# GpSimd builds the local keys' block-diagonal tiles unit by unit; first stacks by row half; 32-column value tiles; fewer warm-up matmuls

## The chip, the cores and the metric

One core of a Trainium2 chip, one launch. The metric is device time in microseconds. TensorE's clock has two levels, 2.4 and 1.2 GHz; the profile gives the granted share of the higher one.

## The reference

Two branches over four batches of 512 tokens, 128 wide, are added. The first is a chunked attention: 16 heads of 8, windows of 16 tokens, once over neighbouring tokens and once over every third token ("dilated", three residues), summed and projected:

```python
attn = softmax(einsum('bhqd,bhkd->bhqk', q, k) * SCALE)      # inside each window of 16
out = einsum('bhqk,bhkd->bhqd', attn, v)
return _linear(local_out + atrous_out, Wo, bo)
```

The second is a transformer block: low-rank attention over all 512 tokens, causal, 16 heads of 8 (half of each head rotated by position), then a shared expert and seven routed ones, of which each token takes two, as dense matmuls with weights:

```python
scores = where(causal, einsum('bqhd,bkhd->bhqk', qq, kk) * scale, -inf)
y = einsum('bhqk,bkhd->bqhd', softmax(scores), v) @ W_o
combined = einsum('tei,eih,te->th', silu(g) * u, Wd_r, wts) ; out = shared + combined
```

The kernel lays both into one stream of work and adds the results into `x`.

## The kernel before

The program is a list of steps that `plan()` builds; each engine walks the whole list and issues its own part of each step, so the list is the order of every queue. `merged()` interleaves several lists by the positions in `SPREAD`: a list with the range (lo, hi) has its items laid evenly between, and one unit is about one batch of scores. Semaphores between the parts do the rest.

*Front.* Batch 0 is led by `LN`, `WF` (folds two small weight matrices), `XT` (transpose of x), `MA`/`MB` (keys, side 0, and queries, side 1, of the full attention; `MB` is the turned half of the rotation, which VectorE multiplies and adds, L964 and L967), `ST`. `WARM` puts matmuls on a spare bank ahead of `WF`, `XT` and `MA`, two TensorE instructions each (L1182).

*Stacks.* A bf16 score is made exact by splitting q and k into three bf16 parts (L695 to L722: casts on ScalarE, VectorE or GpSimd, subtractions), and stacking products of parts along the 128 rows: rows 0 to 47 hold the terms of heads 0 to 7, rows 64 to 111 those of heads 8 to 15. SyncE stores the parts to DRAM with a broadcast, twelve DMAs a batch (three parts, two sides, two row halves, L576), and loads `k_stack` and `q_stack` back in `ST` (L587), 112 rows of 8 KB each. Batches alternate between two buffers.

*Scores.* Four groups of four heads a batch, eleven units each. `S` computes scores for the row maxima into a bank of ring A (two banks), drained by VectorE (L1000, L1004); after a group `SHIFT` puts the maxima into the stack. Two groups later `E` computes the shifted transposed scores into ring B (three banks), ScalarE takes the exponential (L823), and `PV` multiplies by the values: four heads side by side, head m in the 32 rows of bank_c from 32m, with 8 value columns and one of ones (L1265). `Y`, `YT`, `X1` take the result on.

*Local attention.* 34 pairs of windows are worked in five units of 8, 8, 8, 8 and 2. `LK`, `LQ`, `LV` project; GpSimd spreads k into `k_part` (L663, L665) and q into `q_part` (L679, L681). `k_diag` holds for each pair the keys times a head mask, eight masks x 1088 columns x two sides. In the `KD` steps VectorE makes four of the eight (L986) and ScalarE four (L772), each for all pairs, once the last `LS` of the batch before is done. `LS` multiplies q_part by k_diag into ring A, VectorE subtracts the maximum (`LS`, L1018 and L1021), ScalarE takes the exponential (`LR`), then `PT` transposes, `LO` multiplies by v_diag (loaded by `VD`), `LT` transposes back and `LW` projects.

*Norm and experts.* `R2` to `PICK` normalise and route; 32 expert steps `GU`/`DOWN` follow the scores. `late` reuses k_diag for their weights, loaded in `WX`.

The wait at the head of `LS` is for all of k_diag and q_part:

```python
if step[2] == 0:
    pe.wait_ge(k_diag_by_dve, KD_PARTS * (b + 1))
    pe.wait_ge(k_diag_by_act, KD_PARTS * (b + 1))
    pe.wait_ge(q_part_ready, KD_PARTS * (b + 1))
```

## Time and profile before

| | us |
|---|---|
| median of 3 runs | 449.01 |
| lowest, highest | 445.97, 450.13 |
| the profiled execution | 444.97 |
| its span in the profile | 443.2 |

The profile is of one execution. Its page gives busy time by engine, the span in 40 slices, the DMA queues, the chain of work that ended last, and the costliest groups of instructions; the trace answers for any stretch: a timeline, the waits, the chain, and windows with busy time and granted clock. PE is TensorE (PEld its weight loads), DVE VectorE, ACT ScalarE, POOL GpSimd, SP SyncE. The line numbers are those of the kernel above. An fp32 matmul is two TensorE instructions in the trace.

### The profile page before, as it was taken

How to read it: one execution, taken by the hardware profiler on the slowest of the kernel's cores; microseconds unless marked ns; L12 is line 12 of the kernel's file. 1: busy time of each engine (PE TensorE's matmuls, PEld its weight loads, DVE VectorE, ACT ScalarE, POOL GpSimd, SP SyncE). 2: the span in 40 equal slices, each digit the busy share in tenths (PEclk: the TensorE clock that was granted, in tenths of full speed). 3: DMA queues.
4: the chain of work that ended last, by engine and by line, in shares of the span. 5: the costliest groups of instructions: out<-in, count | busy, mean ns of one | idle time of the engine just before them, and what ended most of it. 6: DMA issues, size and time to landing. Idle time of an engine off the chain costs nothing.

```text
span 443.2 us, 11906 instructions
## 1 busy us (share of the span) xinstructions
PE 373.1 (84%) x4572; PEld 221.7 (50%) x4572; DVE 295.7 (67%) x854; ACT 224.9 (51%) x472; POOL 127.6 (29%) x148
## 2 busy tenths in 40 slices
PE   6834878885999969797987988889899999998894
PEld 6422635442466535364543654464443566655563
DVE  5865768794687896767879785866731345856542
ACT  5260227353566474464547544455544565566363
POOL 6374036263000354500336000000200235744244
PEclk9975989899899997999999996998955999999899
DMA  8274011036111116202037101230000000000000
GB/s 246 86 210 133 7 30 43 23 134 178 30 63 36 39 39 206 51 12 80 18 111 201 31 7 32 58 89 1 5 1 1 0 0 25 1 27 0 0 25 24
DMA packets 27390, 25.52 MB, mean 58 GB/s; under 512 B 11876, under 2 KB 25444, under 8 KB 26372
## 3 DMA queue, kind: packets, MB, share of 16 engines
q1 hardware_dynamic: 27336, 24.78, 19.4%
q8 instruction: 37, 0.61, 0.6%
q14 instruction: 17, 0.14, 0.1%
HBM read 14.64 MB, written 10.52 MB: 57 GB/s over the span
## 4 chain that ended last, share of the span: by engine, by line
PE 57%; DVE 24%; issue 9%; DMA 3%; ACT 3%; SPq 1%; POOL 1%; DVEq 0%; ACTq 0%
PE bank_B L1358 11%; PE bank_c L1265 8%; PE bank_B L1168 7%; PE bank_A L1364 6%; DVE differences L1000 6%; PE bank_A L1304 4%; PE bank_B L1174 3%; DVE s_loc L1021 2%; DVE row_max L1018 2%; PE bank_M L1211 2%; PE bank_M L1312 2%; DMA q_stack<-parts_dram 2%; PE bank_c L1182 2%; PE bank_M L1327 2%; DVE neg_max L1004 2%
## 5 line engine op out<-in xcount | busy, mean ns | idle before, releaser
L823 ACT ACTIVATE p_mla<-bank_B 128x512 f32<-128x512 f32 (+1 forms) x176 | 97.2, 561 | 94.1 <-PE bank_B L1174 92.9
L1000 DVE CUSTOM_DVE_ANT_0 differences<-masks,bank_A 128x512 bf16<-128x512 bf16 (+1 forms) x128 | 78.9, 616 | 32.6 <-PE bank_A L1151 23.6
L1168 PE MATMUL bank_B<-q_stack,k_stack 50*128 50x512 bf16 (+3 forms) x256 | 68.9, 324 | 25.8 <-DVE s_loc L1021 8.2
L1151 PE MATMUL bank_A<-k_stack,q_stack 48*128 48x512 bf16 (+3 forms) x256 | 66.3, 316 | 14.9 <-DMA q_stack<-parts_dram 11.0
L1358 PE MATMUL bank_B<-xrT,k_diag 128*128 128x512 f32 x128 | 64.0, 620 | 3.0 <-DVE k_diag L1129 3.0
L707 POOL TENSOR_TENSOR x<-x,q_part 128x512 f32<-128x512 f32 x32 | 40.7, 1273 | 79.5 <-ACT q_part L857 45.4
L1168 PEld LDWEIGHTS bank_B<-q_stack,k_stack 50*128 50x128 bf16 x256 | 20.1, 97 | 81.0 <-issue 41.7
L1174 PE MATMUL bank_B<-masks 64*128 64x64 bf16 (+1 forms) x512 | 54.0, 212 | 0.0
L1265 PE MATMUL bank_c<-p_mla,v_mla 128*9 128x128 f32 (+3 forms) x512 | 51.7, 479 | 0.7 <-ACT p_mla L823 0.4
L1174 PEld LDWEIGHTS bank_B<-masks 64*128 64x128 bf16 x512 | 42.8, 101 | 15.6 <-issue 4.0
L1129 DVE SCALAR_TENSOR_TENSOR k_diag<-k_diag,bank_B 128x512 f32<-128x512 f32 x32 | 22.0, 687 | 41.7 <-ACT k_diag L841 41.3
L857 ACT ACTIVATE q_part<-bank_A,expert_w 128x128 f32<-128x128 f32 x112 | 32.1, 370 | 30.3 <-PE bank_A L1364 30.3
L1364 PEld LDWEIGHTS bank_A<-k_diag 128*128 128x128 f32 x256 | 33.7, 195 | 14.8 <-issue 14.7
L1004 DVE TENSOR_REDUCE neg_max<-bank_A 128x2 f32<-128x512 f32 (+1 forms) x48 | 32.4, 687 | 8.6 <-PE bank_A L1159 7.8
L1364 PE MATMUL bank_A<-k_diag 128*128 128x128 f32 x256 | 34.6, 279 | 0.7 <-DVEq L1137 0.7
L621 POOL TENSOR_TENSOR nrm<-nrm,half 128x4 f32<-128x4 f32 (+2 forms) x6 | 10.0, 1658 | 82.6 <-DVE nrm L1080 79.8
L1358 PEld LDWEIGHTS bank_B<-xrT,k_diag 128*128 128x128 f32 x128 | 22.3, 197 | 21.0 <-issue 15.3
L719 POOL CAST parts<-rot 128x512 bf16<-128x512 f32 x6 | 4.1, 681 | 92.8 <-DVE rot L967 87.7
L1151 PEld LDWEIGHTS bank_A<-k_stack,q_stack 48*128 48x128 bf16 x256 | 18.7, 94 | 20.4 <-DMA q_stack<-parts_dram 11.2
L1134 DVE TENSOR_TENSOR k_diag<-bank_B,k_diag 128x512 f32<-128x512 f32 x32 | 22.1, 691 | 2.1 <-PE bank_B L1358 1.1
L1327 PE MATMUL bank_M<-v_diag,pT_loc 128*32 128x72 f32 x1088 | 22.9, 228 | 0.1
L1304 PE MATMUL bank_A<-k_diag,q_part 128*32 128x128 f32 x544 | 22.2, 300 | 0.5 <-DVE neg_max L1000 0.4
(149 smaller groups left out, 611.5 us busy)
## 6 DMA issues: line engine op xcount, KB each, us to landing
k_stack<-parts_dram SPq DMA_DIRECT2D x4, 896.0 KB, 7.2
q_stack<-parts_dram SPq DMA_DIRECT2D x4, 896.0 KB, 8.4
parts_dram<-parts SPq DMA_DIRECT2D x16, 192.0 KB, 2.4
v_dram<-v_rows SPq DMA_DIRECT2D x4, 648.0 KB, 4.1
parts_dram<-parts SPq DMA_DIRECT2D x16, 128.0 KB, 2.2
v_diag<-v_dram SPq DMA_DIRECT2D x32, 45.0 KB, 2.1
v_diag<-v_dram SPq DMA_DIRECT2D x32, 36.0 KB, 1.9
x<-in_x SPq DMA_DIRECT2D x4, 256.0 KB, 6.4
```

The source lines that it names most:

```text
L707: link(nc.gpsimd.tensor_tensor(x[:, tb, :], x[:, tb, :], weighted[down_no[step] % 2], ALU.add))
L823: drained_by(nc.scalar.activation(p_of(n)[:, m:m + len(heads), 0:w], src, ACT.Exp, scale=SCALE), step)
L857: ins = nc.scalar.activation(weighted[n % 2][:, i, :], down[:, i, :], ACT.Copy, scale=expert_w[:, c * NT + i, e - 1:e])
L1000: drained_by(nc.vector.tensor_tensor_reduce(differences[:, 0:w], masked16[:, S - w:], bank[:, 0:w], -1.0, -NEG, ALU.add, ALU.min, dst), step)
L1004: drained_by(nc.vector.tensor_reduce(dst, src, AX.X, ALU.max, negate=True), step)
L1151: return nc.tensor.matmul(bank_of(step)[:, n * w:(n + 1) * w], q_stack[b % 2][rows, h % 8, i * P:(i + 1) * P], k_stack[b % 2][rows, h % 8, ...
L1168: nc.tensor.matmul(bank_of(step)[:, m * w:(m + 1) * w], k_stack[b % 2][rows, h % 8, j * P:(j + 1) * P], q_stack[b % 2][rows, h % 8, j * P: ...
L1174: return nc.tensor.matmul(bank_of(step)[:, m * w:m * w + SLOT * (low + 1)], half_eye[half_of(4 * g), low, :], half_causalT[half_of(4 * g), ...
L1265: last = nc.tensor.matmul(bank_c[32 * m:32 * m + HD + 1, j * P:], v_mla[:, b % 2, j, 4 * g + m, :], p_of(n)[:, m, 0:S - j * P], start=(j = ...
L1304: last = nc.tensor.matmul(bank[PAIR * j:PAIR * j + PAIR, c:c + P], q_part[:, a, pair, :], k_diag[:, a, :, CHUNK * pair:CHUNK * pair + CHUN ...
L1358: full_by(nc.tensor.matmul(bank_of(use)[:], w_exp[:, e, m, :], x2T[:, c, :], start=True, stop=True), use)
L1364: last = nc.tensor.matmul(bank[:, i * D:(i + 1) * D], hid[n % 2][:, i * P:(i + 1) * P], w_exp[:, e, 2, :], start=True, stop=True)
```

## The change

- The first stacks: batch 0's stores go out in the order written below, and each stack is loaded in two halves, rows 0 to 63 in `ST 0`, the rest in a new step `ST2` after the last `LV` of batch 0; scores wait for the upper half (`upper_in`) from the third group on.
- From batch 1 on, the block-diagonal tiles are made by GpSimd in steps `KU(b,k)`, one for each unit, each as soon as `LS(b-1,k)` has read the old ones; `LS(b,k)` waits for its own. q_part is made in two steps `QD` (neighbouring, dilated). `KD` is left in batch 0 alone.
- The add of the rotation (L967) is GpSimd's from batch 1 on, in front of its split.
- `PV` uses stationary tiles of `PV_WIDTH` = 32 columns (the next heads' values fill the rows that nobody reads), narrower only at the end of the row for the last three heads.
- 12 instead of 56 warm-up instructions; the clearing of pT_loc moves behind batch 0's bias add; new positions in `SPREAD`.

```diff
-WARM = {("WF",): 14, ("XT", 0, 1): 8, ("MA", 0, 0): 6}
+WARM = {("WF",): 6}
...
-    "scores": [(-0.425, 4.13)],
-    "local": [(-0.415, 0.151), (0.682, 1.537), (1.566, 2.55), (2.462, 3.111)],
-    "project": [(-0.241, 0.196), (0.2, 1.358), (1.405, 2.134)],
-    "stacks": [(-0.922, -0.922), (0.514, 0.514), (1.48, 1.48), (2.141, 2.141)],
-    "values": [(-2.253, -2.253), (0.262, 0.262), (1.367, 1.367), (3.099, 3.099)],
-    "norm": [(1.467, 1.901), (2.152, 2.731), (3.484, 3.677), (4.411, 4.977)],
-    "experts": [(3.974, 5.368)],
-    "statistics": [(-1.535, -1.535)],
+    "scores": [(-0.374, 4.13)],
+    "local": [(-0.216, 0.445), (0.405, 1.245), (1.418, 2.322), (2.432, 3.229)],
+    "project": [(-0.303, 0.196), (0.38, 1.129), (1.609, 2.2)],
+    "stacks": [(-0.955, -0.955), (0.515, 0.515), (1.113, 1.113), (2.221, 2.221)],
+    "values": [(-2.111, -2.111), (0.293, 0.293), (1.494, 1.494), (2.046, 2.046)],
+    "norm": [(1.467, 1.768), (2.121, 2.653), (3.622, 4.014), (4.338, 4.715)],
+    "experts": [(4.075, 5.103)],
+    "spreads": [(0.232, 0.532), (0.558, 1.703), (1.912, 2.578)],
+    "statistics": [(-0.503, -0.503)],
...
-            if k == NLU - 1:
-                steps += [("KD", b + 1, n) for n in range(KD_PARTS)] if b + 1 < B else [("WX",)]
+            if k == NLU - 1 and b + 1 == B:
+                steps.append(("WX",))
...
+    def spreads(b):
+        steps = []
+        for k in range(NLU):
+            steps.append(("KU", b, k))
+            if k in (LOCAL_UNITS - 1, NLU - 1):
+                steps.append(("QD", b, int(k == NLU - 1)))
+        return steps
...
+                if step == ("ST", 0):
+                    for side, part, hp in ((0, 0, 0), (0, 0, 1), (0, 1, 0), (0, 2, 0), (1, 0, 0), (1, 1, 0), (1, 2, 0)):
+                        if part < 2:
+                            sp.wait_ge(rounded[side], part + 1)
+                        else:
+                            sp.wait_ge(split_ready, side + 1)
+                        store(0, side, part, hp)
+                    sp.wait_ge(rows_out, 16 * 4)
+                    sp.wait_ge(parts_out[0][0], 16 * 3)
+                    load(0, 0, slice(0, SLOT), stacks_in[0])
+                    for part in (1, 2):
+                        store(0, 0, part, 1)
+                    sp.wait_ge(parts_out[1][0], 16 * 3)
+                    load(0, 1, slice(0, SLOT), stacks_in[0])
+                if kind == "ST2":
+                    for part in range(3):
+                        store(0, 1, part, 1)
+                    for side in range(2):
+                        sp.wait_ge(parts_out[side][1], 16 * 3)
+                        load(0, side, slice(SLOT, SLOT + SHIFT_ROW), upper_in)
...
+                if step[0] == "KU":
+                    _, b, k = step
+                    wait_full(pool, ("LS", b - 1, k))
+                    if k == 0:
+                        pool.wait_ge(heads_in, 16)
+                        pool.wait_ge(k_part_ready, b + 1)
+                    pairs = LUNITS[k][0]
+                    c = slice(CHUNK * pairs[0], CHUNK * (pairs[-1] + 1))
+                    w = c.stop - c.start
+                    for a in range(2):
+                        ins = nc.gpsimd.tensor_tensor(k_diag[:, a, :, c],
+                                                      k_part[:, a, c].unsqueeze(1).broadcast_to((P, X, w)),
+                                                      head_mask[:].unsqueeze(2).broadcast_to((P, X, w)), ALU.mult)
...
                 if step[0] == "MB" and step[1] > 0:
...
-                    pool.wait_ge(rot_ready, n)
+                    whole = rot[:, side, :]
+                    wait_drained(pool, ("MA", b, side))
+                    wait_drained(pool, step)
+                    link(nc.gpsimd.tensor_tensor(whole, whole, turned[b][:], ALU.add))
+                    pool.sem_inc(rot_ready, 1)
...
+                    heads = v_mla[:, b % 2, j].rearrange("p h d -> p (h d)")
                     for m in range(4):
-                        last = nc.tensor.matmul(bank_c[32 * m:32 * m + HD + 1, j * P:], v_mla[:, b % 2, j, 4 * g + m, :],
+                        first = (HD + 1) * (4 * g + m)
+                        width = min(PV_WIDTH, H * (HD + 1) - first)
+                        last = nc.tensor.matmul(bank_c[32 * m:32 * m + width, j * P:], heads[:, first:first + width],
...
-                    if step[2] == 0:
-                        pe.wait_ge(k_diag_by_dve, KD_PARTS * (b + 1))
-                        pe.wait_ge(k_diag_by_act, KD_PARTS * (b + 1))
-                        pe.wait_ge(q_part_ready, KD_PARTS * (b + 1))
+                    if b:
+                        pe.wait_ge(k_diag_by_pool, NLU * (b - 1) + step[2] + 1)
+                    elif step[2] == 0:
+                        pe.wait_ge(k_diag_by_dve, KD_PARTS)
+                        pe.wait_ge(k_diag_by_act, KD_PARTS)
+                    if step[2] in (0, LOCAL_UNITS):
+                        pe.wait_ge(q_part_ready, 2 * b + (2 if step[2] else 1))
```

In the new list `KU(1,0)` is ahead of the eighth score unit of batch 0's third group, `LS(1,0)` after the third of the fourth; `MB(1,0)` and `MB(1,1)` stand at the end of the second group and after the second unit of the third; `KU(3,1)`, `MB(3,0)` and, some three units on, `MB(3,1)` follow each other at the turn of batch 2's second and third group. The first `GU` comes after all `E`.

## Rows read from the trace of the kernel before

**Rows 1.** The page: busy time, chain by engine, one DMA issue line
```profile
PE 373.1 (84%) x4572; PEld 221.7 (50%) x4572; DVE 295.7 (67%) x854; ACT 224.9 (51%) x472; POOL 127.6 (29%) x148
PE 57%; DVE 24%; issue 9%; DMA 3%; ACT 3%; SPq 1%; POOL 1%; DVEq 0%; ACTq 0%
q_stack<-parts_dram SPq DMA_DIRECT2D x4, 896.0 KB, 8.4
```

**Rows 2.** Timeline to the first scores: start, duration, engine, line, operation [idle before]
```profile
18.12 8.88 SPq L576 DMA_DIRECT2D parts_dram<-parts  x12
35.40 0.17 DVE L886 TENSOR_TENSOR nrm<-mv,nrm 128x12 f32<-128x12 f32 x1
37.35 1.03 PE L1151 MATMUL bank_A<-k_stack,q_stack 48*128 48x512 bf16 x2 [11.01 <-DMA q_stack<-parts_dram]
38.00 0.69 DVE L1000 CUSTOM_DVE_ANT_0 differences<-masks,bank_A 128x512 bf16<-128x512 bf16 x1 [2.43 <-PE bank_A L1151]
```

**Rows 3.** Timeline at the front: warm-up matmuls and VectorE ahead of WF
```profile
3.97 5.39 PE L1182 MATMUL bank_c<-eye 128*128 128x128 f32 x28 [3.97 <-DMA eye<-in_c_eye]
8.87 1.11 DVE L945 TENSOR_SCALAR xr<-x,mv,nrm 128x128 f32<-128x128 f32 x4
```

**Rows 4.** Timeline: two waits of TensorE, and a KD multiply beside GpSimd's split
```profile
163.36 1.76 DVE L986 TENSOR_SCALAR k_diag<-k_part,head_mask 128x1088 f32<-128x1088 f32 x1
110.76 0.58 PE L1168 MATMUL bank_B<-q_stack,k_stack 50*128 50x512 bf16 x1 [4.65 <-issue]
180.21 0.37 PE L1168 MATMUL bank_B<-q_stack,k_stack 50*128 50x512 bf16 x1 [1.87 <-issue]
```

**Rows 5.** Chain of waits by line, first 66 to 77 us, then 228 to 244
```profile
by line: DVE k_diag L986 25.5%; DVE neg_max L1004 14.3%; issue 10.9%; PE bank_M L1289 9.8%; PE bank_M L1206 9.6%; DVE differences L1000 6.7%; ACT pT_loc L805 6.0%; PE bank_M L1312 5.5%; PE bank_A L1304 4.1%; DVE row_max L1018 3.9%; DVE s_lo
...
by line: DVE differences L1000 19.8%; DVE k_diag L986 15.0%; issue 14.1%; DVE neg_max L1004 11.7%; PE bank_c L1265 8.8%; DVE xn L1088 3.4%; DVE xn L1080 3.3%; PE bank_B L1168 3.1%; DVE s_loc L1021 2.7%; DVE nrm L1085 2.5%; PE bank_M L1336 2
```

**Rows 6.** Windows: stretch, length, busy PE, PEld, DVE, ACT, POOL, granted clock, DMA, GB/s
```profile
28.00:36.00 8.00, 0.00 (x0) 0.00 (x0) 7.43 (x31) 4.79 (x5) 5.40 (x9) 0.54 0.97 268
110.70:115.00 4.30, 4.24 (x27) 1.57 (x27) 2.03 (x7) 2.14 (x4) 0.00 (x0) 0.61 0.00 0
162.70:166.20 3.50, 0.00 (x0) 0.00 (x0) 3.47 (x9) 0.88 (x2) 3.27 (x4) 0.86 0.01 1
166.20:172.00 5.80, 5.73 (x31) 3.00 (x31) 1.95 (x9) 1.99 (x6) 2.48 (x5) 0.50 0.39 136
302.00:320.00 18.00, 15.43 (x222) 7.71 (x218) 14.50 (x48) 11.70 (x23) 2.29 (x2) 1.00 0.01 3
322.00:342.00 20.00, 20.00 (x108) 7.99 (x106) 4.87 (x29) 9.15 (x17) 0.00 (x0) 0.51 0.01 1
```

**Rows 7.** Groups by line and shape: GpSimd's multiply, copy, subtract; two weight loads
```profile
L1304 PEld LDWEIGHTS bank_A<-k_diag,q_part 128*32 128x32 f32 x544 | 16.6, 120 | 5.0 <-issue 2.1 <-DVE neg_max L1000 1.9
L720 POOL TENSOR_TENSOR rest<-rot,parts 128x512 f32<-128x512 f32 x6 | 7.0, 1159 | 0.5
L1265 PEld LDWEIGHTS bank_c<-p_mla,v_mla 128*9 128x9 f32 x512 | 7.7, 89 | 7.4 <-ACT p_mla L823 1.6 <-issue 0.8
L681 POOL COPY q_part<-qT 64x288 f32<-64x288 f32 x8 | 5.7, 718 | 0.5
L643 POOL TENSOR_TENSOR xr<-xn,nrm 128x512 f32<-128x512 f32 x3 | 3.1, 1039 | 23.2 <-issue 22.5 <-POOL parts L722 0.7
```

**Rows 8.** Chain of waits: by line 322 to 342 us, pieces there, two at full clock
```profile
by line: PE bank_c L1265 32.3%; PE bank_B L1168 30.7%; PE bank_B L1358 18.6%; PE bank_B L1174 15.7%; PE bank_M L1272 5.2%
...
335.21 1.82 PE bank_c L1265 x8
338.58 3.71 PE bank_B L1358 x4
...
99.66 0.98 PE bank_c L1265 x8
247.55 0.92 PE bank_A L1304 x32
```

More of the change, by code:

```diff
@@ L57 @@
 P_RING = 2
+PV_WIDTH = 32
 PT_RING = 1
@@ L235, in plan @@
     steps = first[:1] + [("WF",)] + lead + [("ST", 0)]
-    steps += [step for step in first[1:] if step not in lead] + [("KD", 0, n) for n in range(KD_PARTS)]
+    rest = [step for step in first[1:] if step not in lead]
+    after = 1 + max(n for n, step in enumerate(rest) if step[0] == "LV")
+    rest.insert(after, ("ST2", 0))
+    steps += rest
+    steps += [("KD", 0, n) for n in range(KD_PARTS)] + [("QD", 0, n) for n in range(2)]
     at = SPREAD
@@ L249, in plan @@
     assert all(at["PICK", b] < at["DOWN", b, 1] and at["X1", b] < at["R2", b] for b in range(B))
+    assert all(at["LQ", b] < at["KU", b, 0] and at["LS", b - 1, k] < at["KU", b, k] < at["LS", b, k]
+               for b in range(1, B) for k in range(NLU))
+    assert all(at["LS", b - 1, (LOCAL_UNITS - 1, NLU - 1)[n]] < at["QD", b, n] < at["LS", b, (0, LOCAL_UNITS)[n]]
+               for b in range(1, B) for n in range(2))
+    assert all(at["KU", b - 1, NLU - 1] < at["LK", b] and at["QD", b - 1, 1] < at["LQ", b] for b in range(2, B))
     return steps
@@ L438, in build @@
         v_zeroed, v_rows_set = sem("v_zeroed"), sem("v_rows_set")
-        parts_out = [sem(f"parts_out{side}") for side in range(2)]
+        parts_out = [[sem(f"parts_out{side}{hp}") for hp in range(2)] for side in range(2)]
+        upper_in = sem("upper_in")
         rows_out = sem("rows_out")
@@ L524, in load_x, with store, load @@
                 sp.dma_start(x[:, b * NT:(b + 1) * NT, :], xv[:, b]).then_inc(x_in[b], 16)
+            def store(b, side, part, hp):
+                terms = STORES[side][part]
+                nt = len(range(*terms.indices(TERMS)))
+                to = parts_dram[b % 2, side, hp, 0:SHIFT_ROW, :].rearrange("(t d) (a n) -> (d a) t n", d=HD, n=S)
+                sp.dma_start(to[:, terms, :], parts[hp::2, side, part:part + 1, :]
+                             .broadcast_to((SLOT, nt, S))).then_inc(parts_out[side][hp], 16)
+            def load(b, side, rows, done):
+                dst = (q_stack if side else k_stack)[b % 2]
+                src = parts_dram[b % 2, side].rearrange("h r n -> (h r) n")
+                sp.dma_start(dst[rows].rearrange("p a n -> p (a n)"), src[rows, :]).then_inc(done, 16)
             load_x(0)
@@ L573, in _ @@
[L573 removed]
                         for hp in range(2):
[L575 to L578 removed]
+                            store(b, side, part, hp)
@@ L579, in _ @@
+                if kind == "ST" and b:
                     if b >= 2:
                         wait_full(sp, ("E", b - 2, GROUP_ORDER[-1], NT - 1, 0))
-                    else:
-                        sp.wait_ge(rows_out, 16 * 4)
                     for side in range(2):
-                        sp.wait_ge(parts_out[side], 16 * 6 * (b + 1))
-                        dst = (q_stack if side else k_stack)[b % 2]
-                        src = parts_dram[b % 2, side].rearrange("h r n -> (h r) n")
-                        sp.dma_start(dst[0:SLOT + SHIFT_ROW].rearrange("p a n -> p (a n)"),
-                                     src[0:SLOT + SHIFT_ROW, :]).then_inc(stacks_in[b % 2], 16)
+                        for hp in range(2):
+                            sp.wait_ge(parts_out[side][hp], 16 * 3 * (b + 1))
+                        load(b, side, slice(0, SLOT + SHIFT_ROW), stacks_in[b % 2])
@@ L767, in _ @@
                         act.wait_ge(heads_in, 16)
[L768 to L770 removed]
+                        act.wait_ge(k_part_ready, 1)
                     x = KD_PARTS + n
@@ L964, in _ @@
                     drained_by(nc.vector.tensor_tensor(dst, bank[:], rope[:, which, :], ALU.mult), step)
-                    if which:
+                    if which and b == 0:
                         wait_drained(dve, step)
@@ L1222, in _ @@
                         pe.wait_ge(stacks_in[b % 2], STACK_IN * (b // 2 + 1))
+                    if b == 0 and step[2] == 2 * PER_GROUP:
+                        pe.wait_ge(upper_in, STACK_IN)
                     if step not in waits_for_e:
```

80 lines of the change are left out of this document (40 added, 40 removed).

## The prediction

> **What bounds the kernel now.** I read the page's busy line, its chain, then windows of 2 to 20 us, the waits of TensorE, and the timeline around each. TensorE is busy 84% of the span and makes up 57% of the chain, VectorE 24% [rows 1]: no engine is full, and the order of the steps decides. The reader should see four kinds of loss. (a) Start: TensorE stands 11.01 us until q_stack lands and first works at 37.35; VectorE's first drain of a score bank is at 38.00 [rows 2]. (b) At the first scores of batches 1 and 2 TensorE waits 4.65 and 1.87 us [rows 4]; the row names no releaser, but these are the moments at which the q_stack loads of 8.4 us land [rows 1]. (c) The four `KD` steps put 1088 columns eight times into the queues of VectorE and ScalarE, between score banks that TensorE waits for. `KD` on VectorE is 25.5% of the chain from 66 to 77 us and 15.0% from 228 to 244 [rows 5]; in the third batch's stage TensorE does nothing for 3.5 us beside a busy VectorE and then runs 5.8 us at granted clock 0.50 (1.2 GHz) [rows 6]. (d) The end of the scores: from 322 to 342 TensorE is busy 20.00 of 20.00 us at a clock of 0.51, ScalarE only 9.15 [rows 6], and the chain there names no other engine [rows 8]. The experts behind it are dense TensorE work at full clock, and the change takes nothing from them.
>
> **Part by part.** Sums are against the profiled execution, 444.97 us with a span of 443.2; the median shown is 449.01, so I carry the difference over to it.
>
> *First stacks by row half.* Twelve stores are issued one after the other for 8.88 us, then two loads of 112 rows (896 KB); q_stack's lands at 37.3 [rows 1, 2]. Afterwards only seven stores go ahead of the lower k half (64 rows, 512 KB) and two more ahead of the lower q half. At 8.88 / 12 = 0.74 us an issue lower q is reached near 18.12 + 10 x 0.74 = 25.5 and waits for its stores to land, I take 26.5; 1.0 MB at the 268 GB/s of that stretch [rows 6] is 3.8 us, landed near 31 to 32. The remaining three stores, v_dram and the upper halves (heads 8 to 15, needed from group 2) lie behind, under some 20 us of scores. But VectorE is not free: `KD` and `STATS 0` keep it until 35.57 [rows 2]. So the first drain moves from 38.00 to 35.6: **-2.4 us** (0 to -4).
>
> *Warm-up matmuls.* 44 of 56 instructions go. The 28 ahead of `WF` took 5.39 us, but VectorE's own work ahead of `WF` runs to 9.98 [rows 3], so `WF` is drained only some 0.5 us earlier; the 28 later ones stood between it and `MA`, which can start about 2 us earlier, possibly at 1.2 GHz, where each `MA`/`MB` costs 0.86 us more. **0** (-2 to +1).
>
> *Stacks of batches 1 and 2.* `MA`/`MB` of batch 1 move from group 2 to the turn of groups 1 and 2 of batch 0, and `ST 2` forward by more than a group. The 4.65 us wait should go, with the slow stretch after it (4.24 us of work at 0.61, worth 1.7 at full clock), and the 1.87 us wait too [rows 4, 6]. -6.3 and -1.9.
>
> *Block-diagonal tiles.* Twelve `KD` steps leave VectorE and ScalarE. What they cost on the chain is 0.255 x 11 = 2.8 us and 0.150 x 16 = 2.4 us in two stages [rows 5], and in the third 3.5 us idle plus half of 5.8 us at half clock, 6.4 [rows 6]. -11.6. The second half of `MB`'s rotation (one add in six steps) also leaves VectorE. GpSimd gets per full unit two multiplies of 8 x 128 elements per partition. No row has them; the nearest is its 512-element multiply with a broadcast operand, 1039 ns, 2.0 ns an element, the high bound its copy of 288 elements at 718 ns, 2.5 [rows 7]. I take the multiply: 2 x 1024 x 2.03 = 4.2 us a full unit (high 5.1), 18 us a batch, 54 in all. GpSimd is at 29% (127.6 us), and in the score stages mostly waits.
>
> *What the new work can hold up.* `LS(b,k)` on TensorE now waits for its own unit, with all scores queued behind it. The tightest place is batch 1: between `KU(1,0)` and `LS(1,0)` stand seven to eight score units, at (320 - 37) us / 176 units = 1.6 us each about 12 us, against 4.2 + 4.2 + four q copies of at most 0.72, 11.3 us: 0 to +5, I take +1. In batch 3 `KU(3,1)` stands just ahead of `MB(3,0)` on GpSimd, whose add and split are three two-input instructions of 1.16 us and two casts, I take 5 us [rows 7]; VectorE waits for that split in `MB(3,1)` about three units later, with score drains behind it. 4.2 + 5 less 5 us: +3 (0 to +4).
>
> *Wider value tiles.* The stationary side goes from 9 to 32 columns; the moving columns are as before. A 9-column weight load takes 89 ns, a 32-column one 120 ns [rows 7]: 0 to 8 x 31 ns x 64 `PV` = 16 us. In `LS` 32 matmuls of 128 columns with 32-column loads take 0.92 us together [rows 8], so the loads hide; near the low end, +1. What it may bring is loss (d). A `PV` of 512 queries takes 0.98 us at full clock and 1.82 in the slow stretch; the clock came back only after one `GU` step, four instructions with 128-column weights, 3.71 us at half clock [rows 8]. I forecast that with 32-column tiles this stretch runs at 1.0. Then its 16.4 us of E and PV (322.1 to 338.5) fall to about 11 (half is 8.2, but ScalarE needs about 9 and TensorE would wait for it), and 3.7 us of `GU` to 1.9: **-7.3** (0 to -9).
>
> The Trainium skill ("TensorE: Matmul & The Clock Gate", Part 1 and the goals table) holds that keeping TensorE busy without gaps releases the clock. In this row a TensorE without a gap stays at 0.51, so the trace disagrees; by that rule the width of a tile buys nothing, which is the rival "the clock stays low", 434 us. The skill's "SBUF — State Buffer" (contention rules) says that a GpSimd instruction that reads SBUF locks out VectorE instructions in a two-port mode, and this speaks against the change. The trace has a `KD` multiply of 1.76 us beside GpSimd's split [rows 4], and agrees as far as that goes; by the rule some of the 28 normalising multiplies of VectorE would be held up by as much as one GpSimd multiply, 2 us.
>
> **Sum.** Mid stages -6.3 - 1.9 - 11.6 = -19.8, of which I keep three quarters, -15, since time given free is partly taken by the next wait (VectorE is busy 14.50 of 18 us there [rows 6]). With the local work of batch 0 laid more evenly I add -2. -2.4 - 15 - 2 - 7.3 + 1 + 1 + 3 = -21.7. 444.97 becomes 423.3; on the median 449.01, **427 us**.
>
> **Rivals.**
> *The freed engines buy little.* TensorE is the pace wherever it isn't idle; only its idle gaps with their slow stretches go, 6.3 + 1.9 + 6.4, and half comes back elsewhere, while batch 0's local work, pushed back, costs about 6 us of TensorE time later. For it: busy 15.43 of 18 us at full clock [rows 6]. -2.4 - 7 + 6 - 7.3 + 5 = -6: 443. If the clock doesn't rise either, 449.
> *No net change:* that case, within 1%.
> *Slower: GpSimd becomes the pace.* Place: `KU` in batches 1 to 3. From `KU(1,0)` to `LS(1,4)` lie about 35 units, 56 us, less about 15 us of GpSimd's other work; five units fit up to 8 us each. At 12 us a unit (5.9 ns an element) TensorE stands about 20 us more a batch, net +25 with the gains: 474; it decides from 8 us on, and 10 us gives about 455. Against it: the three GpSimd rows shown cost 2.0 to 2.5 ns an element [rows 7].
> *The clock stays low:* 427 + 7 = 434. For it: nothing in this trace shows a wide `PV`.
> *More than forecast:* all mid gains kept and the stages more even, 415.
>
> **Chances.** Forecast (420 to 432) 0.40; clock stays low, 434, 0.17; more than forecast, 415, 0.18; freed engines buy little, 443, 0.08; no change 0.09; slower 0.08. The predicted time is the likeliest case's. The range takes in the three cases next to it and leaves out the ends: 412 to 443. About 1% is what a measurement of this kernel can tell from no change: faster 0.82, within 1% 0.10, slower 0.08.
>
> **What would show it.** First drain of a score bank near 35.6; no TensorE wait above 1 us at the first S of batches 1 and 2; `KU` multiplies near 2.1 us; no long wait of TensorE for GpSimd's k_diag at `LS`, and a VectorE wait of some 3 us at `MB(3,1)`; granted clock near 1.0 and a 512-query `PV` near 1 us between the last S and the first GU. Wrong it would be if GpSimd's multiplies take over 4 us, if the slow stretches only move, or if the wider loads show between the value matmuls.

## The result, and the profile after

The changed kernel takes **432.02 us** (median of 4 runs, 428.61 to 433.03), the kernel before 449.57 in the same comparison (445.97 to 451.45): a ratio of **0.961**, 95% interval 0.952 to 0.969. The profiled execution took 432.39 us, its span is 430.6. Set against the profiled execution of before the gain is only 12.6 us, since that one (444.97) was among the quicker ones. Over all comparisons of this study the kernel before ran 54 times, from 436.30 us at a mean granted clock of 0.929 to 452.96 at 0.906, and the changed one 10 times with a median of 431.8. The difference of the means is 15.0 ± 2.0 us (2.2 standard errors, as wherever "±" stands below). So differences of 2 to 3 us between two kernels here are at the edge of what can be told. The experiments ran in four sets on four chips, in which the kernel before had medians of 448.0, 449.1, 447.9 and 444.3; the changed kernel itself ran again only in the second, so a difference between two sets carries more than its "±". Where only the fast executions count (within 1.5% of a kernel's fastest in the set), the ratio to the kernel before is 0.985 (0.978 to 0.992) for batch 2's normalisation alone, 1.004 (0.997 to 1.011) for the other places alone and 1.016 (1.006 to 1.025) for wide value tiles alone.

The page of the changed kernel, busy time and chain by engine:

```profile
PE 365.3 (85%) x4528; PEld 220.1 (51%) x4528; DVE 287.7 (67%) x836; ACT 211.3 (49%) x460; POOL 181.5 (42%) x184
PE 56%; DVE 17%; issue 6%; ACT 4%; POOL 3%; DMA 2%; SPq 2%; DVEq 0%; ACTq 0%; POOLq 0%
```

Beside [rows 1]: GpSimd has 53.9 us more and VectorE's share of the chain fell from 24% to 17%; but VectorE is only 8.0 us less busy. Twelve multiplies of `KD` and six adds of the rotation are gone from it: by the groups of both kernels these lines took 15.6 + 4.1 us, and 3.5 are left of them, 16.2 us less. Half of that came back, most of it in three groups whose number of instructions is the same: the multiplies of `LN` take 6.7 instead of 4.6 us, those of `R3` 6.5 instead of 5.7, the `rt` products of `PICK` 4.5 instead of 2.5.

The start, in the timeline of the changed kernel:

```profile
32.12 1.03 PE L1219 MATMUL bank_A<-k_stack,q_stack 48*128 48x512 bf16 x2 [6.43 <-DMA q_stack<-parts_dram]
34.55 0.68 DVE L1068 CUSTOM_DVE_ANT_0 differences<-masks,bank_A 128x512 bf16<-128x512 bf16 x1
35.30 0.61 PE L1219 MATMUL bank_A<-k_stack,q_stack 48*128 48x512 bf16 x1 [2.15 <-DVE neg_max L1068]
```

TensorE starts 5.2 us earlier than in [rows 2], VectorE's first drain comes 3.45 earlier, and TensorE then waits 2.15 us for VectorE, as forecast.

From the first drain to the last S the two kernels take nearly the same time. The windows of before and of the changed kernel (start, end, length, then busy PE, PEld, DVE, ACT, POOL, the granted clock, DMA share, GB/s):

```profile
38.00:315.70 277.70, 234.88 (x3786) 137.51 (x3787) 209.00 (x615) 141.05 (x277) 61.02 (x84) 0.94 0.22 62
```

```profile
34.55:311.30 276.75, 238.00 (x3785) 142.08 (x3787) 200.17 (x589) 127.98 (x264) 116.49 (x119) 0.92 0.24 64
```

Idle TensorE went from 42.8 to 38.8 us, but busy TensorE rose by 3.1 at a lower clock. Behind the last S lie 127.5 us before and 119.3 after. So in these two executions the end gave 8.2 us, the start 3.4, and the middle, where the change does most and where 13 us net were forecast, 1.0.

What stands in the middle instead are new waits. The groups by line and shape of the changed kernel:

```profile
L727 POOL TENSOR_TENSOR k_diag<-k_part,head_mask 128x1024 f32<-128x1024 f32 x24 | 45.6, 1899 | 2.5 <-POOLq L716 0.5 <-POOL q_part L750 0.2 <-POOL x L690 0.2
L1020 DVE TENSOR_SCALAR xn<-x,mv,nrm 128x128 f32<-128x128 f32 x12 | 6.7, 622 | 0.0
```

and its timeline at two places:

```profile
92.32 4.50 DVE L1020 TENSOR_SCALAR xn<-x,mv,nrm 128x128 f32<-128x128 f32 x4
92.62 3.87 POOL L727 TENSOR_TENSOR k_diag<-k_part,head_mask 128x1024 f32<-128x1024 f32 x2 [0.18 <-POOL q_part L750]
97.35 1.47 PE L1380 MATMUL bank_A<-k_diag,q_part 128*32 128x128 f32 x32 [3.31 <-DVE neg_max L1068]
...
193.21 7.88 POOL L727 TENSOR_TENSOR k_diag<-k_part,head_mask 128x1024 f32<-128x1024 f32 x4 [0.27 <-POOLq L716]
193.25 1.90 DVE L1187 TENSOR_TENSOR rt<-rt 128x32 f32<-128x32 f32 x1
196.16 0.39 PE L1236 MATMUL bank_B<-q_stack,k_stack 50*128 50x512 bf16 x1 [3.05 <-DVE neg_max L1072]
```

The reader should see an instruction of VectorE that takes many times its length while GpSimd multiplies: the four normalising multiplies of `LN 2`, 1.11 us together elsewhere ([rows 3] has the same work at the front), take 4.50; the small `rt` product of `PICK 0`, 0.19 us undisturbed (e1_hold, below), takes 1.90, which is one `KU` multiply (1899 ns). The score drains queue behind, and TensorE stands 3.31 and 3.05 us. Behind the second wait it runs slowly, by the windows:

```profile
196.00:200.00 4.00, 3.28 (x45) 2.05 (x49) 3.23 (x11) 2.19 (x4) 3.84 (x3) 0.61 0.14 28
200.00:210.00 10.00, 10.00 (x122) 5.64 (x118) 3.56 (x11) 4.74 (x10) 1.09 (x1) 0.64 0.01 2
```

The Trainium skill ("SBUF — State Buffer", the contention rules) says that a VectorE instruction with two SBUF inputs contends with a GpSimd instruction that reads SBUF. The `rt` product is such a one, and this trace agrees with 1.90 against 0.19 us.

### The profile page after: what moved, and what is told of

Read it like the earlier page. It is cut to its first block, busy times and chain, and to the rows that moved or that the text cites. A ratio compares the mean times of both kernels' runs of the same rounds, so it can differ in the third digit from the quotient of the medians.

```text
span 430.6 us, 11866 instructions
## 1 busy us (share of the span) xinstructions
PE 365.3 (85%) x4528; PEld 220.1 (51%) x4528; DVE 287.7 (67%) x836; ACT 211.3 (49%) x460; POOL 181.5 (42%) x184
## 4 chain that ended last, share of the span: by engine, by line
PE 56%; DVE 17%; issue 6%; ACT 4%; POOL 3%; DMA 2%; SPq 2%; DVEq 0%; ACTq 0%; POOLq 0%
PE bank_B L1434 12%; PE bank_c L1338 7%; PE bank_A L1440 6%; PE bank_B L1236 6%; DVE differences L1068 4%; PE bank_A L1380 4%; PE bank_M L1403 3%; PE bank_M L1279 2%; ACT p_mla L893 2%; PE bank_M L1388 2%; PE bank_B L1242 2%; PE bank_M L1274 2%; PE bank_M L1362 1%; PE bank_M L1269 1%; PE bank_A L1219 1%
## 5 line engine op out<-in xcount | busy, mean ns | idle before, releaser
L1236 PE MATMUL bank_B<-q_stack,k_stack 50*128 50x512 bf16 (+3 forms) x256 | 65.5, 310 | 16.4 <-DVE neg_max L1068 5.3
L1219 PE MATMUL bank_A<-k_stack,q_stack 48*128 48x512 bf16 (+3 forms) x256 | 67.5, 322 | 11.7 <-DMA q_stack<-parts_dram 6.4
L1434 PE MATMUL bank_B<-xrT,k_diag 128*128 128x512 f32 x128 | 61.7, 603 | 3.3 <-DVE k_diag L1197 3.3
L1242 PE MATMUL bank_B<-masks 64*128 64x64 bf16 (+1 forms) x512 | 51.5, 206 | 0.0
L727 POOL TENSOR_TENSOR k_diag<-k_part,head_mask 128x1024 f32<-128x1024 f32 (+1 forms) x30 | 49.3, 1642 | 2.9 <-POOLq L716 0.5
L1338 PE MATMUL bank_c<-p_mla,v_mla 128*32 128x384 f32 (+13 forms) x512 | 47.7, 446 | 2.0 <-ACT p_mla L893 1.1
L1242 PEld LDWEIGHTS bank_B<-masks 64*128 64x128 bf16 x512 | 40.5, 96 | 14.1 <-issue 2.3
L1072 DVE TENSOR_REDUCE neg_max<-bank_A 128x2 f32<-128x512 f32 (+1 forms) x48 | 32.6, 690 | 10.4 <-PE bank_A L1227 9.5
L784 POOL TENSOR_TENSOR rot<-rot,rest 128x512 f32<-128x512 f32 x6 | 7.6, 1271 | 59.6 <-DVE rest L1034 59.4
L1403 PE MATMUL bank_M<-v_diag,pT_loc 128*32 128x72 f32 x1088 | 24.1, 238 | 1.0 <-DMA v_diag<-v_dram 0.7
```

Source lines behind the costliest of these rows:

```text
L727: ins = nc.gpsimd.tensor_tensor(k_diag[:, a, :, c], k_part[:, a, c].unsqueeze(1).broadcast_to((P, X, w)), head_mask[:].unsqueeze(2).broadc ...
L1219: return nc.tensor.matmul(bank_of(step)[:, n * w:(n + 1) * w], q_stack[b % 2][rows, h % 8, i * P:(i + 1) * P], k_stack[b % 2][rows, h % 8, ...
L1236: nc.tensor.matmul(bank_of(step)[:, m * w:(m + 1) * w], k_stack[b % 2][rows, h % 8, j * P:(j + 1) * P], q_stack[b % 2][rows, h % 8, j * P: ...
L1242: return nc.tensor.matmul(bank_of(step)[:, m * w:m * w + SLOT * (low + 1)], half_eye[half_of(4 * g), low, :], half_causalT[half_of(4 * g), ...
L1338: last = nc.tensor.matmul(bank_c[32 * m:32 * m + width, j * P:], heads[:, first:first + width], p_of(n)[:, m, 0:S - j * P], start=(j == 0) ...
L1403: last = nc.tensor.matmul(bank[PAIR * j:PAIR * j + PAIR, c:c + w], pT_loc[:, t % PT_RING, par, 2 * i + (g ^ par), PAIR * j:PAIR * j + PAIR ...
```

## The experiments

Each is a small edit. Medians are given with lowest and highest; the kernel before ran beside each set. Two theories on the missing middle were set against each other: that GpSimd's multiplies hold VectorE up (called the lock below), and that time freed on VectorE is simply worth little.

**Holding GpSimd back (e1_hold).** Two waits in `KU` on GpSimd:

```
 wait_full(pool, ("LS", b - 1, k))
+if (b, k) == (1, 2):
+    pool.wait_ge(xn_ready, 3)
+if (b, k) == (3, 0):
+    pool.wait_ge(picked, 1)
```

> The changed kernel with two waits more on GpSimd: the tile unit KU(1,2) waits until VectorE has normalised batch 2 (step LN 2), and KU(3,0) until PICK 0 is done. Lock theory (the middle stages gained 0.9 us instead of 13 because GpSimd's tile multiplies hold up VectorE's small SBUF-to-SBUF instructions, 3.31 and 3.05 us of idle TensorE and half-clock stretches behind them): the four multiplies of LN 2 take 1.1 to 1.4 us together instead of 4.50, the rt instruction of PICK 0 0.2 us instead of 1.90, both TensorE waits go, and the time falls by 5 to 9 us, to about 425. Rival (time freed on VectorE is worth little, another wait sets the pace): the instructions get short but the time stays at 431 to 433. Second rival (the slowness has nothing to do with GpSimd): the instructions stay long.

425.59 us (420.45 to 429.60, 6 runs), 6.2 ± 3.1 less than the changed kernel. The timeline of this kernel at the same two places:

```profile
90.62 1.11 DVE L1024 TENSOR_SCALAR xn<-x,mv,nrm 128x128 f32<-128x128 f32 x4
91.88 3.87 POOL L731 TENSOR_TENSOR k_diag<-k_part,head_mask 128x1024 f32<-128x1024 f32 x2 [1.18 <-DVE xn L1024]
92.27 1.08 PE L1384 MATMUL bank_A<-k_diag,q_part 128*32 128x128 f32 x32
...
191.51 0.19 DVE L1191 TENSOR_TENSOR rt<-rt 128x32 f32<-128x32 f32 x1
192.06 7.82 POOL L731 TENSOR_TENSOR k_diag<-k_part,head_mask 128x1024 f32<-128x1024 f32 x4 [0.86 <-DVE expert_w L1193]
192.71 0.39 PE L1240 MATMUL bank_B<-q_stack,k_stack 50*128 50x512 bf16 x1 [1.34 <-DVE neg_max L1076]
```

GpSimd does all of its work, only some of it 1 us later, and it costs nothing there. 1.11 for 4.50 us, 0.19 for 1.90; no wait before the `LS`, and 1.34 for 3.05. From 192 to 207 us the clock is 1.00, where the changed kernel had 0.61 and 0.64 behind the wait, and the last S comes at 303.4 instead of 311.3 us. The lock theory is right, in place and size.

**Without the multiplies (e2_ku_out).** `KU`'s two multiplies replaced by `pool.sem_inc(k_diag_by_pool, 1)`.

> The changed kernel without GpSimd's multiplies in KU (the local keys' block-diagonal tiles stay those of batch 0; the semaphores are still raised), so that 49 us of GpSimd work are gone and nothing takes their place. Lock theory: 8 to 10 us less than the changed kernel, about 423, with no VectorE multiply of LN above 0.5 us. Rival (freed time is worth little): 430 to 432. If GpSimd's own queue were what is late (its split, its q copies): also faster, but then the holding of KU in the other run would not help.

424.03 us (421.49 to 426.63), 7.6 ± 2.6 less than the changed kernel and 1.6 below e1_hold in the median, which can't be told from nothing. So 49 us of GpSimd work cost 6 to 8 us, and all that can be shown of it lies at those two places. This kernel leaves the local keys' tiles of batches 1 to 3 unmade.

**Writing alone (e11_ku_memset).** The multiplies replaced by `nc.gpsimd.memset(k_diag[:, a, :, c], 0.25)`.

> The changed kernel with KU's two multiplies replaced by two memsets of the same slices of k_diag, so GpSimd writes the same bytes and reads nothing; the local attention of batches 1 to 3 is computed from a constant. Lock theory with reading as its cause: the four multiplies of LN 2 take 1.4 us together, 0.34 us each, though a GpSimd memset runs beside them, and the time is that of the kernel without KU multiplies, 424. Rival (any long GpSimd access holds VectorE up, writing too): LN 2's multiplies take as long as the memset beside them lets them, over 2 us together, and 426 to 431.

421.60 us (418.07 to 423.89, 4 runs), not to be told from the run without the multiplies (2.7 ± 3.5 less). The timeline of this kernel at `PICK 0`, then its group of memsets:

```profile
185.22 3.98 POOL L727 MEMSET k_diag<- 128x1024 f32 x4 [0.24 <-POOLq L716]
185.29 0.19 DVE L1185 TENSOR_TENSOR rt<-rt 128x32 f32<-128x32 f32 x1
```

```profile
L727 POOL MEMSET k_diag<- 128x1024 f32 x24 | 22.8, 951 | 1.9 <-POOLq L716 0.5 <-POOL q_part L748 0.2 <-POOL x L690 0.2
```

This is the same `rt` product, begun 0.07 us after GpSimd's first memset of 951 ns: 0.19 us. Beside a multiply it was 1.90. So GpSimd's reading is what holds this instruction up, not its writing. For `LN 2` the run says nothing: there the memsets end at 89.02, before VectorE's multiplies begin at 90.68, so the rival (writing holds such multiplies up too) stays untested.

**Tiles back on VectorE and ScalarE (e3_after_kd).** The step order gets `KD` back in `local`, `KU` goes, and the rotation's add returns to VectorE:

```
-            if k == NLU - 1 and b + 1 == B:
-                steps.append(("WX",))
+            if k == NLU - 1:
+                steps += ([("KD", b + 1, n) for n in range(KD_PARTS)] + [("QD", b + 1, n) for n in range(2)]
+                          if b + 1 < B else [("WX",)])
...
-        lists.append((spreads(b), *at["spreads"][b - 1]))
```

> The changed kernel with the block-diagonal tiles of batches 1 to 3 and the second half of the rotation back on VectorE and ScalarE, everything else (front, order of the other steps, wide value tiles, warm-ups) as changed. Prediction as it stands: +11.6 for the KD steps and nothing back, 444. Lock theory: +11.6 for the KD steps, -6 to -9 for the lock that goes: 435 to 438. Rival (freed engine time is worth little): the lock goes and the KD steps hide, 424 to 429.

441.40 us (439.15 to 446.17), 10.4 ± 2.7 more than the changed kernel and 16.7 ± 3.5 more than e1_hold. The second number is the worth of the tiles without the lock. The prediction as it stands (+11.6) fits the first better than what the lock theory expected (435 to 438): the lock theory had taken 11.6 for the tiles too, and by the second number they are worth more. Where it lies, in windows of this kernel at its second `KD`:

```profile
88.00:92.00 4.00, 2.26 (x24) 0.69 (x21) 3.93 (x7) 4.00 (x6) 3.79 (x4) 0.63 0.02 5
92.00:96.00 4.00, 4.00 (x53) 2.83 (x50) 2.69 (x5) 2.36 (x4) 3.52 (x7) 0.51 0.54 183
```

VectorE and ScalarE are full (3.93 and 4.00 of 4 us), TensorE has 2.26, and then works 4.00 of 4.00 us at clock 0.51: the idle time is paid twice. It need not be. The windows of e9_before_order (below), which has the same four steps at the same moment:

```profile
88.00:92.00 4.00, 3.07 (x62) 2.25 (x66) 4.00 (x7) 4.00 (x5) 3.69 (x6) 1.00 0.52 180
92.00:96.00 4.00, 3.50 (x89) 2.42 (x77) 3.79 (x13) 3.75 (x10) 1.36 (x3) 1.00 0.07 20
```

TensorE finds more to do there beside full VectorE and ScalarE (3.07 of 4 us instead of 2.26), and no slow stretch follows. The two kernels have the same places in the step order up to there; they differ in the front, in the width of the value tiles and in how q_part is made. Which of these lets TensorE work on isn't shown.

**Narrow value tiles (e4_narrow).** `PV_WIDTH = HD + 1` instead of 32 in the changed kernel.

> The changed kernel with value tiles of 9 columns as before, all else as changed. Width theory: granted clock near 0.5 between the last S and the first GU, 512-query PV 1.8 us there, and 7 to 9 us more, about 440. Rival (the clock is up there because of the order or because an idle gap comes earlier or later): clock 1.0 and the time within 1 us of 432.

432.19 us (427.85 to 435.69), 0.6 ± 2.8 more than the changed kernel: nothing. The windows over the end of the scores and the first GU, changed kernel first, then with 9 columns:

```profile
320.00:340.00 20.00, 18.66 (x158) 10.79 (x156) 8.17 (x36) 11.45 (x22) 1.27 (x1) 1.00 0.01 2
```

```profile
320.00:340.00 20.00, 18.80 (x155) 10.97 (x156) 8.79 (x37) 10.89 (x21) 1.27 (x1) 1.00 0.01 2
```

Clock 1.00 in both, where the kernel before had 0.51 in a like stretch [rows 6]. The clock is up, as forecast, but not through the width.

**Wide value tiles alone (e5_before_wide).** The kernel before with the changed `PV` lines and nothing else.

> The kernel before with value tiles of 32 columns and nothing else. The run with 9-column tiles in the changed kernel (432.2 us, granted clock 1.00 between the last S and the first GU) spoke against the width. Width theory (the forecast's step): granted clock about 1.0 from 322 to 342 us and 7 us less than before, 441. Order theory (what lifts the clock in the changed kernel is where batch 2's transposes and router stand): clock about 0.5 there as before, a 512-query PV 1.8 us, time as before, 448 +- 3.

451.64 us (447.76 to 454.28): 4.7 ± 2.5 more than the kernel before over all its runs, 2.6 in the medians of this set. The windows from the last S to the first GU, kernel before first, then with wide tiles:

```profile
315.70:338.50 22.80, 22.16 (x173) 10.37 (x167) 8.01 (x40) 12.10 (x24) 1.58 (x2) 0.64 0.01 1
```

```profile
319.90:342.80 22.90, 22.30 (x173) 10.77 (x167) 8.01 (x40) 12.13 (x24) 1.58 (x2) 0.64 0.01 1
```

Clock 0.64 in both, so the width doesn't lift it. The time lies just above what the order theory allowed (448 ± 3). Why the kernel gets slower by the width is open; the windows show TensorE busy 240.4 of 282.1 us between first drain and last S against 234.9 of 277.7, at 0.92 against 0.94.

**Batch 2's normalisation later (e6_before_norm).** One pair of numbers in the kernel before:

```
-    "norm": [(1.467, 1.901), (2.152, 2.731), (3.484, 3.677), (4.411, 4.977)],
+    "norm": [(1.467, 1.901), (2.152, 2.731), (3.622, 4.014), (4.411, 4.977)],
```

> The kernel before with batch 2's normalisation, transposes, router and PICK at the changed kernel's place (0.14 and 0.34 groups later, after the last S and among the E units), nothing else. Order theory: the stretch between the last S and the first GU runs at a granted clock near 1.0 and the time falls by about 7 us, to 441. Rival (the clock there hangs on what came long before, as on the waits and stages of the whole kernel): clock 0.5 somewhere in the stretch, 448.

438.09 us (437.14 to 438.88): 8.5 ± 1.5 less than the kernel before, the largest gain of any single edit to that kernel. Its window from the last S to the first GU, then its timeline:

```profile
318.50:334.40 15.90, 15.11 (x176) 8.07 (x169) 7.54 (x39) 11.62 (x24) 2.29 (x2) 1.00 0.01 3
```

```profile
328.97 0.66 PE L1201 MATMUL bank_M<-eye,xn 128*128 128x128 f32 x4
331.06 0.96 PE L1347 MATMUL bank_M<-wide,xrT 128*128 128x7 f32 x8
332.30 1.04 PE L1265 MATMUL bank_c<-p_mla,v_mla 128*9 128x512 f32 x8
334.38 1.95 PE L1358 MATMUL bank_B<-xrT,k_diag 128*128 128x512 f32 x4 [0.17 <-ACT p_mla L823]
```

The same work that took 22.8 us at 0.64 takes 15.9 us at 1.00, with 9-column tiles; a `PV` of 512 queries takes 1.04 us and the first GU 1.95, where before they took 1.82 and 3.71 [rows 8]. From the last S to the end it is 117.1 us instead of 127.5. In the kernel before, the transposes (L1201) and the router (L1347) of batch 2 stood at 318.18 and 319.75, just ahead of the fall at 322; here they stand ten microseconds later and no fall follows. In the kernel before TensorE was busy 5.36 of 6 us before the fall, and busy throughout after it. Of that kernel one execution is traced, and 14 of its 54 took no more than 442.8 us: whether its clock falls at 322 us in every one isn't shown.

**The other places (e9_before_order).** The kernel before with the changed kernel's numbers for scores, local, project, stacks, values and statistics; norm of batches 2 and 3 and the experts stay.

> The kernel before with all of the changed kernel's places in the step order (local, project, stacks, values, statistics, first group of scores) except batch 2's and 3's normalisation and the experts, which stay. What is known: the changed kernel with KD put back stands at 441.4 us, and order of the normalisation (-11) and the front (-3.4 at the first drain) would alone give about 434.6. Forecast of the prediction (the 4.65 and 1.87 us waits at the first S of batches 1 and 2 go, and local work lies more evenly): 8 to 10 us less than before, 439 to 441. Theory now (the new places cost more TensorE time at half clock and idle than these waits did, as long as KD sits on VectorE and ScalarE): 452 to 458, although both waits are gone. Between, 447 to 451: the 6.8 us come from the joint, not from the order.

442.57 us (439.36 to 449.51, 12 runs): 3.0 ± 3.2 less than the kernel before in this set, 5.3 in the medians. The theory (452 to 458) fell, and so did the value between. A gain isn't shown clear of noise, and 8 to 10 us, the forecast's size, is too much. In its trace (of the execution of 449.51 us) the wait at the first S of batch 1 is 1.56 us instead of 4.65 [rows 4]. At that of batch 2 there is still one, of 2.12 us for VectorE. The changed kernel has its like; its timeline there:

```profile
173.71 1.21 DVE L1156 TENSOR_SCALAR xn<-x,nrm 128x128 f32<-128x128 f32 x4
174.85 0.68 DVE L1086 TENSOR_REDUCE row_max<-bank_A 128x32 f32<-128x512 f32 x1
175.56 0.69 DVE L1089 TENSOR_TENSOR s_loc<-bank_A,row_max 128x512 f32<-128x512 f32 x1
176.31 0.55 PE L1236 MATMUL bank_B<-q_stack,k_stack 50*128 50x512 bf16 x1 [1.73 <-DVE s_loc L1089]
```

The stacks are there in time now, but VectorE is busy without a gap from `R3 0` to the local maxima just ahead of it, and TensorE waits 1.73 us for VectorE where it had waited 1.87 for the load.

**First stacks whole again (e12_whole).** The changed kernel with twelve stores and two loads of 112 rows:

```
-                    load(0, 0, slice(0, SLOT), stacks_in[0])
-                    for part in (1, 2):
-                        store(0, 0, part, 1)
-                    sp.wait_ge(parts_out[1][0], 16 * 3)
-                    load(0, 1, slice(0, SLOT), stacks_in[0])
...
+                        load(0, side, slice(0, SLOT + SHIFT_ROW), stacks_in[0])
```

> The changed kernel with the first stacks stored and loaded whole as before (twelve stores, then two loads of 112 rows), all else as changed. The forecast's step says +2.4 us (first drain of a score bank back near 38.0 from 34.5, at most +3.5), 434 to 435. Rival (the start at half clock gives it back: the first scores run at 0.50 and TensorE is behind anyway): 431 to 432. Rival (later scores meet the clock in another place, as in the other runs, where single waits cost twice their length): 436 to 440.

433.83 us (429.69 to 435.54), 1.6 ± 2.6 more than the changed kernel, which ran in other sets. Against the kernel before of its own set it is 10.8 ± 4.0 less, where the changed kernel was 15.0 ± 2.0 less, which would make the halves worth 4. The timeline:

```profile
35.83 1.03 PE L1211 MATMUL bank_A<-k_stack,q_stack 48*128 48x512 bf16 x2 [10.80 <-DMA q_stack<-parts_dram]
36.47 0.69 DVE L1060 CUSTOM_DVE_ANT_0 differences<-masks,bank_A 128x512 bf16<-128x512 bf16 x1 [2.51 <-PE bank_A L1211]
```

The drain at 36.47 is 1.92 us later than with halves, and both differences in time are in line with that. In the kernel before it stood at 38.00, so 1.5 of the 3.45 us came from the rest of the front (fewer warm-ups, the memset of `pT_loc` moved); which of them, no run parts.

**Warm-ups in the wait for the stacks (e7_hold_warm).** e1_hold with `WARM = {("WF",): 6, ("S", 0, 0): 40}`.

> The changed kernel with the two GpSimd waits (425.6 us) and 40 warm-up matmuls on the idle TensorE ahead of the first S, while the stacks are still loading. In that kernel the scores run at granted clock 0.50 from 32 to about 49 us and TensorE is busy nearly throughout from 44. If TensorE's idle time ahead of the first S is what holds the clock down: clock 1.0 from 32 us on, last S 2 to 4 us earlier, 422 to 424. Rival (the score units themselves don't keep it up, or VectorE sets the pace there anyway): 425 to 426, and 427 if the extra matmuls delay the first S.

421.31 us (420.21 to 425.03): 3.2 ± 3.2 less than e1_hold, at the edge; against the kernel before of the same set a ratio of 0.950, interval 0.941 to 0.958. It is the fastest kernel of this study that leaves nothing out. Its windows:

```profile
34.00:36.00 2.00, 1.36 (x7) 0.45 (x6) 1.46 (x5) 0.00 (x0) 1.46 (x1) 1.00 0.88 160
36.00:38.00 2.00, 0.72 (x2) 0.18 (x2) 1.71 (x6) 0.00 (x0) 2.00 (x1) 1.00 1.02 119
...
40.00:42.00 2.00, 1.07 (x3) 0.31 (x4) 1.86 (x9) 0.00 (x0) 0.08 (x1) 0.50 0.00 0
```

The clock is 1.00 when the scores begin, but VectorE sets the pace there (TensorE is busy 0.72 of 2 us), and from 40 us on the clock is 0.50 again. The warm-ups take 9.10 us and end at 34.4, so the first S comes 3 us later than in e1_hold. The gain, if it is one, isn't at the start: the first drain is at 34.79 against 34.47.

**Batch 0's local work earlier (e10_hold_warm_local).** e7_hold_warm with `"local": [(-0.415, 0.151), ...` as in the kernel before.

> The kernel with two GpSimd waits and 40 warm-up matmuls (421.3 us), with batch 0's local work at the place that it had before (0.2 to 0.3 of a group earlier). If pushing it back was what cost time (TensorE busy at granted clock 0.50 from 40 to 48 us with nothing but scores, clock 1.00 in the kernel before from 48 us on, where local work lay there): 2 to 4 us less, 417 to 419. Rival (VectorE is what the first scores wait for, and local work there only adds to its queue): 421 to 425.

435.05 us (430.55 to 436.46): 12.2 ± 2.6 more than e7_hold_warm, and neither theory expected it. Its timeline:

```profile
31.19 1.94 PE L1384 MATMUL bank_A<-k_diag,q_part 128*32 128x128 f32 x32 [6.08 <-ACT k_diag L846]
33.06 9.97 PE L1254 MATMUL bank_c<-eye 128*128 128x128 f32 x80
42.96 0.39 PE L1223 MATMUL bank_A<-k_stack,q_stack 48*128 48x512 bf16 x1
43.38 0.69 DVE L1072 CUSTOM_DVE_ANT_0 differences<-masks,bank_A 128x512 bf16<-128x512 bf16 x1 [8.00 <-PE bank_A L1223]
...
101.24 1.93 PE L1384 MATMUL bank_A<-k_diag,q_part 128*32 128x128 f32 x32 [4.51 <-POOLq L757]
```

`LS(0,0)` now stands ahead of the first S, and TensorE waits 6.08 us there for ScalarE's `KD`. The 40 warm-ups come behind it in the queue: they no longer fill that wait but follow it, for 9.97 us, and the first drain is at 43.38 instead of 34.79. So 8.6 us of the loss lie at the start. The stacks were there in time (the lower q half, issued at 26.17, lands 5.0 us later), and without warm-ups TensorE would have been free for the first S at 33.06. The edit doesn't part the place of the local work from the warm-ups, and what an earlier place costs by itself isn't shown. Later TensorE waits 4.51 us at `LS(1,0)` for GpSimd's q copies, which stand behind two units of `KU`; this is the wait that the prediction priced at 0 to +5, and the changed kernel doesn't have it.

**The changed kernel again (e8_after_again).**

> The changed kernel unaltered, for its time beside the others of this set and for a second trace. All theories: 430 to 433 us; the 4.50 us of LN 2's multiplies and the clock 1.00 from 320 to 340 us come back.

431.83 us (427.41 to 434.62, 6 runs); the groups by line show `LN`'s multiplies again at 6.7 us for 12, and the clock from 320 to 340 us is again 1.00. Both traces of the changed kernel show the same.

## Why the prediction was right, and where not

The forecast, 427 us with 412 to 443, holds the 432.0, and faster was right. But one gain was put down to the wrong edit, and that another edit of the same change gave about as much is luck. One loss was named but not counted; it is about the 5 us by which 427 fell short. Point by point, against [rows 1 to 8] as the steps used them.

- **First stacks by half, -2.4.** First drain 34.55 instead of the 35.6 forecast: the bound was read off the end of `STATS 0` in [rows 2], 35.57, and VectorE came there 0.94 us earlier. Undone alone the edit is worth 1.6 ± 2.6, and 1.92 us at the first drain; the other 1.5 of the 3.45 us come from the rest of the front, for which the forecast had nothing. Right within that. Whether local work has to move back for it, no run shows: in e10_hold_warm_local the warm-ups spoil the answer.
- **Warm-ups, 0.** Not undone by itself, so not shown. Forty new ones ahead of the first S gave 3.2 ± 3.2.
- **Stacks of batches 1 and 2, -6.3 and -1.9, and more even local work, -2.** The 4.65 us wait [rows 4] is gone in the changed kernel; the 1.87 one has its like in 1.73 us for VectorE at the same S. The step that failed here is "and the 1.87 us wait too": it asked when the load lands and not what VectorE has just ahead of that S. All order edits but the normalisation gave 3.0 ± 3.2 where 0.75 x 8.2 + 2 = 8.2 were forecast: the sum of these terms is too high, by how much stays open. And the first wait comes back when all ahead of it gets quicker: in e1_hold TensorE waits 3.10 us at the first S of batch 1, so `ST 1` is the next step to move.
- **Tiles off VectorE and ScalarE, -11.6 (of which the sum keeps three quarters, 8.7).** Worth 10.4 ± 2.7 as the change has them. The term was mis-sized all the same: without the lock they are worth 16.7 ± 3.5. What it left out is the slow stretch that can follow a `KD` gap (clock 0.51 from 92 to 96 us in e3_after_kd) at the first two batches; it had counted one only at the third [rows 6].
- **A unit of `KU` 4.2 us, 54 in all.** 1899 ns for 1024 elements, 1.86 ns each where 2.03 was taken from [rows 7]; 3.8 us a unit, 49.3 in all. Right. GpSimd as the pace (the rival on the slow side, from 8 us a unit) was far off, as argued.
- **New waits, +1 at `LS(1,0)` and +3 at `MB(3,1)`.** Neither came in the changed kernel. At `LS(1,0)` TensorE does wait, 3.31 us, but for VectorE's drain behind the held multiplies of `LN 2`; the wait for GpSimd's own work shows only in e10_hold_warm_local (4.51 us). VectorE's waits for GpSimd in the changed kernel are only those for the roots:

```profile
DVE nrm L962 <- POOL nrm L666: 3.0, 2, 1.8
...
DVE nrm L1153 <- POOL nrm L666: 1.1, 1, 1.1
```

- **The lock, "up to 2 us" and not in the sum.** This is the step that failed in the middle: a cost put at nothing in the sum. It cost 6.2 ± 3.1: the price of one held instruction is the GpSimd multiplies beside it (1.90 for one; 3.39 for the four of `LN 2`, 4.50 less 1.11), and on top of it come the drains queued behind and half-clock work (0.61 and 0.64 from 196 to 210). The forecast had seen the sign of it in [rows 4], had put it in a sentence of its own and gone on without. It also named the wrong instructions alone: the 28 multiplies, but not `PICK`'s small product, which cost as much.
- **Wider value tiles, -7.3, and loads, +1.** The stretch did run at clock 1.00 and a `PV` of 512 queries did take 1.05 to 1.07 us, but the width has no part in it: 0.6 ± 2.8 in the changed kernel, and alone it costs 4.7 ± 2.5. The step that failed is the inference from [rows 6, 8] that narrow weights keep the clock down, because it came back after 128-column ones. The same 9-column `PV` runs at full clock in e4_narrow and e6_before_norm. What gave the 8 us at the end (127.5 to 119.3 in the traces) is a line of the diff that the forecast costed at nothing: batch 2's normalisation moved back by 0.14 and 0.34 of a group, alone worth 8.5 ± 1.5. Why the clock falls at 322 us in the one order and not in the other stays open; it is shown that the order decides and not the width: from the last S to the first GU the three traced kernels with the earlier place (before, e5_before_wide, e9_before_order) have 0.59 to 0.64, the eleven traces with the later one 1.00.

Singly, put into the kernel before (order -3.0, normalisation -8.5, width +4.7) or undone in the changed one (first stacks -1.6, tiles -10.4, width nothing), the edits add up to -23.5 to -18.8, where the whole is -15.0 ± 2.0. The errors of five differences are about as large as what is left over, so that the worths don't add isn't shown. The two traces behind a `KD` step (above) only show that the same four steps can be followed by half clock in one kernel and by full clock in another.

## What to carry to other kernels

Before handing work to GpSimd, list VectorE's instructions that read two SBUF operands, or copy and scale from SBUF to SBUF, and what is queued behind them; a wait that keeps GpSimd's long multiplies off those few moments cost nothing and gave 6 us here. When a stretch runs at half clock, don't credit a new tile shape with lifting it; try the order of the small steps ahead of it first, and undo each edit alone before believing a total that came out right. And put warm-up work only where the engine really idles: behind an instruction that waits it comes on top of the wait, as in e10_hold_warm_local (6.08 us of waiting, then 9.97 of warm-ups).
